# Value matmuls of two quads in a row in every second quad of a ViT layer's attention, with the small steps for neighbouring images at other places

## The reference, cut to what matters

```python
h = patches @ W + b + pos_embed                      # 16 images x 1024 tokens x 64
x = layernorm(h)
q, k, v = (x @ Wq + bq), (x @ Wk + bk), (x @ Wv + bv)   # 8 heads of 8
scores = q @ k.T / sqrt(8) + col_bias                # 1024 x 1024 for each head and image
h = h + softmax(scores) @ v @ Wo + bo
x = layernorm(h)
probs = softmax(x @ router_w.T)                      # 8 experts, the best 2 are taken
h = h + x + sum over the 8 experts of combine[e] * (gelu(x @ w1[e] + b1[e]) @ w2[e] + b2[e])
```

## Time and profile before

| what | value |
|---|---|
| time, median of 3 runs | 1344.19 us (1344.11 to 1345.85) |
| profiled execution, its own time | 1349.47 us |
| its span from first to last instruction | 1347.7 us |
| mean granted TensorE clock | 0.992 |
| TensorE busy | 1220.4 us (91%) |
| ScalarE busy | 1048.0 us (78%) |
| VectorE busy | 833.2 us (62%) |
| GpSimd busy | 115.9 us (9%) |
| idle time of ScalarE before exponentials | 58.1 us, 56.1 of it until scores came |

### The profile page before, as it was taken

One profiled execution on the slowest core, in us unless ns is written; L12 is line 12 of the kernel. 1 busy time (PEld: TensorE's weight loads), 2 busy tenths in 40 slices (PEclk: granted clock), 3 DMA queues, 4 the chain that ended last, 5 costly groups with the idle time before them and its releaser, 6 DMA issues. The chain is left out here.

```text
span 1347.7 us, 26121 instructions
## 1 busy us (share of the span) xinstructions
PE 1220.4 (91%) x9409; PEld 367.0 (27%) x9442; DVE 833.2 (62%) x2164; ACT 1048.0 (78%) x1172; POOL 115.9 (9%) x113
## 2 busy tenths in 40 slices
PE   2159999999999999999999999999999979999998
PEld 1022222222232222222222222223222223332332
DVE  8634376766667666656676766667664366555555
ACT  0059999999999999999999999999999953343333
POOL 4300000000100110000000000000010000000000
PEclk9999999999999999999999999999999988999999
DMA  1133131323322331313131313232221011221221
GB/s 44 35 74 73 34 86 35 86 45 78 73 72 62 62 78 47 74 47 81 39 86 35 86 36 85 64 74 65 64 70 42 1 58 40 64 77 55 73 65 43
DMA packets 63141, 81.18 MB, mean 60 GB/s; under 512 B 26960, under 2 KB 27984, under 8 KB 63000
## 3 DMA queue, kind: packets, MB, share of 16 engines
q1 hardware_dynamic: 60828, 78.76, 23.4%
q10 hardware_dynamic: 1916, 0.55, 0.2%
q0 software_dynamic: 256, 0.01, 0.0%
HBM read 41.90 MB, written 37.27 MB: 59 GB/s over the span
## 5 line engine op out<-in xcount | busy, mean ns | idle before, releaser
L1020 ACT ACTIVATE probs<-psum 128x1024 f32<-128x1024 f32 x1024 | 954.1, 1092 | 58.1 <-PE psum L1149 56.1
L1165 PE MATMUL psum<-probs,VA 128*32 128x512 f32 x4096 | 547.1, 605 | 8.0 <-DVE oT L1066 7.3
L1149 PE MATMUL psum<-QA,KA 54*128 54x512 bf16 x2048 | 349.2, 386 | 31.9 <-ACTq L1039 9.4
L1149 PEld LDWEIGHTS psum<-QA,KA 54*128 54x128 bf16 x2048 | 80.3, 93 | 531.1 <-ACT probs L1020 492.7
L1303 ACT ACTIVATE act_h<-psum,b 128x512 f32<-128x512 f32 x128 | 87.8, 687 | 143.5 <-PE psum L1406 138.5
L1354 DVE TENSOR_TENSOR gated<-act_h,psum 128x512 f32<-128x512 f32 x128 | 87.8, 687 | 91.2 <-ACT act_h L1303 91.1
L1165 PEld LDWEIGHTS psum<-probs,VA 128*32 128x32 f32 x4096 | 83.7, 108 | 132.5 <-issue 99.5
L1066 DVE STREAM_TRANSPOSE oT<-psum 128x512 f32<-128x512 f32 x64 | 45.8, 715 | 115.7 <-PE psum L1165 115.1
L1406 PE MATMUL psum<-m_x,w_parts 128*128 128x512 bf16 x367 | 105.0, 393 | 5.6 <-DMA m_cT<-cT_d 3.2
L1378 PE MATMUL psum<-gated,w 128*64 128x512 f32 x256 | 69.9, 624 | 0.0
L1020 ACT ACT_TABLE_LOAD x1 | 1.3, 1283 | 79.4 <-issue 79.4
(11 more groups left out here) (184 smaller groups left out, 1033.8 us busy)
## 6 DMA issues: line engine op xcount, KB each, us to landing
QA<-q_parts_d SPq DMA_DIRECT2D x64, 192.0 KB
KA<-k_parts_d SPq DMA_DIRECT2D x64, 192.0 KB
q_parts_d<-qk_parts SPq DMA_DIRECT2D x32, 192.0 KB, 2.5
k_parts_d<-qk_parts SPq DMA_DIRECT2D x32, 192.0 KB, 2.7
xT<-in_xT SPq DMA_DIRECT2D x16, 256.0 KB, 3.4
q_parts_d<-qk_parts SPq DMA_DIRECT2D x32, 128.0 KB, 2.6
k_parts_d<-qk_parts SPq DMA_DIRECT2D x32, 128.0 KB, 2.6
x_d<-x_stacks SPq DMA_DIRECT2D x16, 256.0 KB, 2.1
```

What stands on the lines that cost most here:

```text
L1020: nc.scalar.activation(probs[:, k % PROB_BUFS, :], score_buf(buf_of(k)), ACT.Exp).then_inc(exped, 1)
L1149: last = pe.matmul(score_buf(buf_of(k))[:, (g % 2) * BANK:(g % 2 + 1) * BANK], KA[rows_of(h, SCORE_ROWS), h // 2, jt * P:(jt + 1) * P], QA ...
L1165: last = pe.matmul(o_acc[32 * g:32 * g + 32, :], VA[:, jt, h, :], probs[:, k % PROB_BUFS, (g % 2) * BANK:(g % 2 + 1) * BANK], start=(jt == ...
```

## The change

The value matmuls are issued in odd quads only: after the scores and the small steps of odd quad q come the values of quads q-3 and q-2. In even quads only scores and small steps are issued. Several small steps, the router's exponential and the ranking of experts get other places: `v` from slot 11 to 12, `out_proj` from 18 to 16, `flag` from 19 to 18, `post_t0` and `post_t1` from 23 and 24 to 21 and 22, `router` from 25 to 24, `combine_t` from 31 to 30. `EVAC_SLOTS` and the order in `body` on VectorE are as before.

```diff
-AUX_SLOTS = {2: ["embed"], 7: ["norm_t0"], 8: ["norm_t1"], 9: ["qk0"], 10: ["qk1"], 11: ["v"], 14: ["sq"],
-             18: ["out_proj"], 19: ["flag"], 23: ["post_t0"], 24: ["post_t1"], 25: ["router"], 31: ["combine_t"]}
+AUX_SLOTS = {2: ["embed"], 7: ["norm_t0"], 8: ["norm_t1"], 9: ["qk0"], 10: ["qk1"], 12: ["v"], 14: ["sq"],
+             16: ["out_proj"], 18: ["flag"], 21: ["post_t0"], 22: ["post_t1"], 24: ["router"], 30: ["combine_t"]}
-ROUTER_EXP_BLOCK = 52
+ROUTER_EXP_BLOCK = 50
-COMBINE_SLOT = 26
+COMBINE_SLOT = 25
                             aux_step(step, b + 1 if step in PREP else b - 1, aux_base(b) + i + 1, aux_base(b) + i)
-                        if q >= LAG:
+                        if q % 2 and q >= LAG:
+                            values(b, q - LAG - 1)
                             values(b, q - LAG)
-                        elif not first:
+                        elif q % 2 and not first:
+                            values(b - 1, QUADS + q - LAG - 1)
                             values(b - 1, QUADS + q - LAG)
```

## The result

The changed kernel takes 1504.78 us (median of 4 runs, 1502.53 to 1505.63) against 1344.15: a ratio of 1.119, 95% interval 1.1171 to 1.121, +160.6 us. The forecast was 1528, range 1475 to 1560, slower with 0.95.

What follows compares the result with a forecast made beforehand. TensorE (91% busy) and ScalarE (78%) were taken as nearly balanced. To the median of 1344.2 us came 136 for the wait, pair loop and small steps and 48 for the clock: 1528 us, range 1475 to 1560.

Steps and rivals of the forecast that it cites:

- The wait for evacuation 1: Quad 16's values in slot 19 wait for VectorE, which does `out_proj` before evacuation 1: 8.6 us an image.
- T12: The moment when the first scores of slot 12 are issued, from which the prediction counts VectorE's chain.
- The pair loop: An even and an odd quad together take 3.68 us, where ScalarE alone would take 3.67; no slack.
- D: Last of a pair's four score blocks; all the pair's values stand behind it, starting 0.32 us after it.
- two saved changes of shape: Fewer switches of TensorE's array between scores and values: 0.2 us a pair by the tiling rule alone.
- The small steps: Per image: `embed` +1.08 us, `norm_t0`, `qk0` and `post_t0` in odd slots +1.85 in full, `combine_t` +0.67.
- The clock: TensorE's clock falls to 0.50 after each wait for evacuation 1: 3.2 us an image, +48 us in all.
- The clock at 1.00: Rival: the wait comes but the clock stays up, or falls for less than a quad: 1480 us, chance 0.13.
- The rival in which the wait does not come at all: VectorE reaches evacuation 1 in time, or the order is other than read: 1354 us, chance 0.06.
- The faster rival: Saved shape changes shorten the four value passes behind D, below 1.82 us: about 1336 us, chance 0.03.

Runs made afterwards that it cites:

- e2: The changed kernel with one quad's values in each quad, as before the change; only the small steps have their new places: 1.1186, 1507.8 us.
- e5: The changed kernel without the addition that ends VectorE's part of `out_proj` (result lacks the residual): 1.1121, 1499.47 us.
- e3: The changed kernel with VectorE doing evacuation 1 first and its part of `out_proj` right behind it, TensorE's order untouched: 1.0915, 1471.77 us.
- e1: The kernel before the change with the values of two quads together in odd quads, small steps at their old places: 1.0391, 1401.59 us.
- e4: The changed kernel with 36 unused matmuls on TensorE in slot 19 before the values, in images 1 to 14: 1.0987, 1481.32 us.
- e9: Kernel e1 with `v` in slot 12 instead of 11: 1.0351, 1396.68 us.
- e8: Kernel e3 with VectorE's part of `flag` right behind the first addition of `out_proj` instead of behind all of it: 1.0763, 1451.78 us.

## Why the prediction was right

- **The wait for evacuation 1** came where and as forecast. From the first scores of slot 12 to the values of quad 16 I had 22.98 us and to slot 20 24.84 plus 1.75 for the clock; counted from the row of `v_new` (242.31, forecast at 1.44 after T12), the values start 21.26 later (forecast 21.54), and slot 20 at 24.83 (forecast 25.15). e2 shows that the new places alone make the loss, and e5 agrees with the chain counting one to one. That it is VectorE's order, e3 shows: the wait vanished with an edit on VectorE alone.
- **The pair loop** of 3.68 us, with 1.86 for two quads' values: confirmed; twelve exponentials are at full pitch, and in e1 two quads' values start 3.69 and 3.68 us apart (444.39, 448.08, 451.76). e1 shows the other side of it: without slack, each step or wait behind D is paid in full, +53 us. The 0.2 us a pair that the prediction gives for two saved changes of shape was not in its sum; the rows have 0.14 (1.86 against 2 x 1.00).
- **The small steps.** `norm_t0` 0.47, `qk0` 0.78 and `post_t0` 0.47 us of idle time and some 0.1 of lost overlap each: 0.55, 0.75 and 0.55 were forecast. `embed` lost 0.23 and 0.45, with overlap 0.9, for 1.08; `combine_t` 0.46, about 0.55, for 0.67.
- **The clock** fell, as forecast, but this term was mis-sized: 3.2 us an image in the sum, 1.95 by e4. I took 7.5 us at the low clock after work begins, from the start of the attention; it was 4.8. That is 15 x 1.25 = 19 of the 23 us by which 1528 is too high. The rest is of the size of the tenths above.
- **The rivals.** The clock at 1.00 would have been 1480; e4, where it stays, has 1481 (1477 on the first chip's scale). The rival in which the wait does not come at all (1354) is refuted. Its price was probably too low as well: e1 has waits for drains of `aux` that I had left out, but at the old places, so no run shows the price at the new ones. The faster rival needed 1.82 us for the four passes; they took 1.86.

My own expectations failed in one way three times (e1, e3, e9): I followed a step's input and not the drain of the step before it from the shared bank, which stands in VectorE's order wherever that step was put. The prediction left these drains out too. In the changed kernel one of them, 0.75 us before `flag` in slot 18, falls inside the wait for evacuation 1, which ends when VectorE is done, so it cost nothing. That part was luck.

## What to carry to other kernels

A step placed in one engine's written order is also placed in every other engine's: before moving it, write down what then stands ahead of what on each queue, and which engine waits for the thing that is now behind. Where a shared bank passes from step to step, count the drain of the step before as well as the input. Grouping work to save changes of the array's shape takes away slack; with three score buffers the loop from one exponential to the next became about as long as ScalarE's own time (3.68 and 3.67 us), so that a short wait that had been partly hidden was paid in full. Cutting a long step in two and spreading it was worth more (0.9%) than grouping.

## What the runs showed of the hardware

In e8 the granted clock fell to 0.50 within a wait of only 2.95 us on TensorE, when some 2 us of it were over; a wait of 2.11 us shortly ahead of it had left it at 1.00. In the next image of the same run the same wait of 2.11 us (before `flag`, until 328.61) was followed by 0.50. So these rows give no length of wait that is safe. Windows of e8 (columns as in the earlier trace rows):

```profile
263.00:264.00 1.00, 0.00 (x0) 0.00 (x0) 0.93 (x3) 1.00 (x2) 0.00 (x0) 0.95 0.02 5
264.00:265.00 1.00, 0.07 (x2) 0.10 (x3) 0.97 (x4) 0.28 (x1) 0.00 (x0) 0.50 0.04 12
...
330.00:332.00 2.00, 2.00 (x12) 0.39 (x8) 1.73 (x13) 1.31 (x2) 0.60 (x1) 0.50 0.89 208
```

And the low clock lasted 4.8 us after work began again in the changed kernel and about 5.5 us in e2 (from 267.37), where at the start of the attention it had lasted until the end of 7.5 us of unbroken work from 84.02, with shorter pieces of work since 79.83: one stretch is a poor measure of another. At that start the low level is read from durations alone, since the column of the granted clock has 1.00 from 84 to 91.5 us. The last slow quad of values takes 1.58 us to the next scores, where 1.00 is usual:

```profile
90.29 1.65 PE L1165 MATMUL psum<-probs,VA 128*32 128x512 f32 x8
91.87 0.61 PE L1149 MATMUL psum<-QA,KA 54*128 54x512 bf16 x4
```
